# A recommendation tower on one core: another order for the first look-ups, table copies and grams, and a cap on the tables in flight

## The reference

```python
# dense_ctx (2048, 16), ids (2048, 27), tbl_f (1000 to 125000, 128), all float32
e = jnp.stack([tbl_0[ids[:, 0]], ..., tbl_26[ids[:, 26]]], axis=1)      # (2048, 27, 128)
dot_products = jnp.einsum('bnd,bmd->bnm', e, e)
z = dot_products[:, c, r]                   # the 351 pairs below the diagonal
h = jnp.concatenate([z, dense_ctx], axis=1)                             # (2048, 367)
h = jnp.maximum(h @ W_top1 + b_top1, 0.0)                               # 512 wide
h = jnp.maximum(h @ W_top2 + b_top2, 0.0)                               # 256 wide
y = h @ W_top3
```

## Time and profile before

| what | value |
|---|---|
| median of 3 runs | 360.65 us (360.56 to 360.74) |
| the profiled execution | 360.54 us |
| its span, first to last instruction | 358.7 us |
| TensorE busy | 333.7 us, 93% |
| VectorE, ScalarE, GpSimd busy | 246.3, 144.4, 250.4 us |
| mean granted TensorE clock | 0.986 of full speed |
| DMA moved | 36.86 MB |

### The profile page before, as it was taken

One profiled execution on the slowest core, in us unless ns is written; L12 is line 12 of the kernel. 1 busy time (PEld: TensorE's weight loads), 2 busy tenths in 40 slices (PEclk: granted clock), 3 DMA queues, 4 the chain that ended last, 5 costly groups with the idle time before them and its releaser, 6 DMA issues.

```text
span 358.7 us, 13616 instructions
## 1 busy us (share of the span) xinstructions
PE 333.7 (93%) x6094; PEld 303.4 (85%) x6094; DVE 246.3 (69%) x329; ACT 144.4 (40%) x265; POOL 250.4 (70%) x271
## 2 busy tenths in 40 slices
PE   1879699989999989999999999999999999999896
PEld 0779499978999979898889989999899989997775
DVE  3959979975488935878197965968387955961142
ACT  2536524444433433335343453435343353435320
POOL 5777777777777777777777777777777777777200
PEclk9969989999999999999999999999999999999999
DMA  6997744534333353443333452434533443322100
GB/s 184 306 318 196 205 136 107 102 93 91 83 93 82 90 99 75 96 96 80 93 88 82 115 85 77 105 84 81 102 89 83 99 98 74 84 55 55 27 3 1
DMA packets 26155, 36.86 MB, mean 103 GB/s; under 512 B 8451, under 2 KB 20099, under 8 KB 26098
## 3 DMA queue, kind: packets, MB, share of 16 engines
q0 software_dynamic: 8448, 17.32, 20.5%
q1 hardware_dynamic: 17506, 18.16, 20.1%
q10 hardware_dynamic: 144, 0.52, 0.4%
HBM read 35.97 MB, written 0.01 MB: 100 GB/s over the span
## 4 chain that ended last, share of the span: by engine, by line
PE 57%; POOL 26%; issue 10%; DVE 3%; DMA 3%; ACT 1%; DVEq 0%; ACTq 0%
POOL rows L450 26%; PE e_banks L482 25%; PE w_banks L543 9%; PE g_banks L513 8%; PE w_banks L554 7%; PE e_banks L494 6%; DMA rows<-in_tbl,idx 2%; DVE one_hot L672 2%; PE w_banks L532 1%; DVE zt L686 1%; DMA idx<-in_idx 1%; ACT et L340 0%; ACT h L333 0%; ACT et L350 0%; DVE a L720 0%
## 5 line engine op out<-in xcount | busy, mean ns | idle before, releaser
L450 POOL DMA_INDIRECT rows<-in_tbl,idx x264 | 249.6, 945 | 82.9 <-issue 78.0
L672 DVE TENSOR_TENSOR one_hot<-ids_wide,row_no 128x1024 fp32r<-128x1024 int32 x160 | 186.3, 1215 | 76.5 <-PE e_banks L482 72.5
L482 PE MATMUL e_banks<-one_hot,table_hi 128*128 128x256 f32 x672 | 172.2, 294 | 3.4 <-issue 3.4
L482 PE MATMUL e_banks<-one_hot,table_lo 128*128 128x256 f32 x672 | 167.0, 287 | 0.0
L482 PEld LDWEIGHTS e_banks<-one_hot,table_hi 128*128 128x128 f32 x672 | 131.4, 196 | 4.4 <-issue 4.2
L482 PEld LDWEIGHTS e_banks<-one_hot,table_lo 128*128 128x128 f32 x672 | 131.6, 196 | 0.2
L350 ACT ACTIVATE et<-e_banks 128x256 f32<-128x256 f32 x84 | 57.9, 689 | 89.3 <-PE e_banks L482 89.3
L340 ACT ACTIVATE et<-e_banks 128x512 f32<-128x512 f32 (+1 forms) x68 | 45.0, 664 | 52.3 <-PE e_banks L494 51.5
L513 PEld LDWEIGHTS g_banks<-et 128*26 128x26 f32 x4096 | 41.7, 103 | 17.7 <-issue 13.3
L513 PE MATMUL g_banks<-et 128*26 128x26 f32 x4096 | 50.0, 191 | 1.8 <-DVE zt L686 1.3
L494 PE MATMUL e_banks<-ident,rows 128*128 128x128 f32 x264 | 43.0, 285 | 5.5 <-DMA rows<-in_tbl,idx 5.5
(11 more groups left out here) (25 smaller groups left out, 67.7 us busy)
## 6 DMA issues: line engine op xcount, KB each, us to landing
ids_wide<-in_ids SPq DMA_DIRECT2D x80, 128.0 KB
et<-in_kept_tables SPq DMA_DIRECT2D x10, 512.0 KB, 10.1
rows<-in_tbl,idx POOLq DMA_INDIRECT x264
et<-in_kept_tables ACTq DMA_DIRECT2D x1, 512.0 KB, 3.9
a1T<-in_ids SPq DMA_DIRECT2D x4, 128.0 KB, 10.8
w<-in_w SPq DMA_DIRECT2D x2, 256.0 KB
w<-in_W_top SPq DMA_DIRECT2D x1, 512.0 KB
w<-in_w SPq DMA_DIRECT2D x1, 222.0 KB
```

What stands on the lines that cost most here:

```text
L450: pool.indirect_dma_start(rows[:, k % RING, a, :], None, tables[f], bass.IndirectOffsetOnAxis(ap=idx[:, t, f:f + 1], axis=0)).then_inc(row ...
L482: last = nc.tensor.matmul(e_bank[n % E_BANKS][:, 0:UNIT], part[:, q, c, :], one_hot[:, hot_slot(o, piece), c % PIECE, :], start=(c == 0 an ...
L672: nc.vector.tensor_tensor(one_hot[:, hot_slot(o, piece), :, :], ids_place(o).unsqueeze(1).broadcast_to([P, PIECE, UNIT]), row_no[:, piece ...
```

## The change

The six later look-ups of unit 0 are spread over the ticks 0 to 4, so the first of them now stands before chunk 1. The copy of the last table (HI 10) is moved out of the first look-ups to tick 6, behind half of tile 0's grams; it lies in `w_banks`, and the grams of tile 0 wait for the remainder of table 8, the last that reads `g_banks`, and no longer for a zeroed bank: the memset is gone. The grams of tile 0 stand in the ticks 5 and 6 instead of 6 to 9, and the look-ups of unit 1 move behind them. SyncE waits before table n until table n - 2 has landed. GpSimd waits before chunk k until chunk k - `ahead` is transposed, with `ahead` 3 for the first four chunks, 4 for the next four, and so on up to 7.

```diff
+LEAD_AT_FIRST = 3
...
     for n, q in enumerate(looked_up(0)):
-        at = 1 + (n - AHEAD) * 7 // 10
-        step = [("OH", 0, q)] + [("HI", n + AHEAD)]
-        if n == FIRST_LOOK_UPS - 1:
-            step += [("HI", m) for m in range(n + AHEAD + 1, NOH)]
+        step = [("OH", 0, q)] + ([("HI", n + AHEAD)] if n + AHEAD < NOH - 1 else [])
         if n < AHEAD:
             FIRST += step
         else:
-            look_ups[at].append(step)
+            look_ups[(n - 1) * 2 // 3].append(step)
+    look_ups[TILE_AT[1] + 1].append([("HI", NOH - 1)])
 
     for t in range(LAST_TILE):
-        at = TILE_AT[t + 1] + (t == 0)
+        at = TILE_AT[t + 1]
+        ticks = 2 if t == 0 else 4
         for p in range(G_PIECES):
...
-            grams[at + p * 4 // G_PIECES].append(step)
+            grams[at + p * ticks // G_PIECES].append(step)
...
-        hi_banks = [g_banks, w_banks]
+        hi_banks = [w_banks if n == NOH - 1 else (g_banks, w_banks)[n % 2] for n in range(NOH)]
+        LAST_IN_G = max(n for n in range(NOH) if hi_banks[n] is g_banks)
...
                     sp.wait_ge(hi_ready, n - STAGES + 1)
+                if n >= 2:
+                    sp.wait_ge(table_in[n - 2], 16)
                 sp.dma_start(stage(n), kept_tables[:, TABLE_ORDER[n], :, :]).then_inc(table_in[n], 16)
...
-                if k >= RING:
-                    pool.wait_ge(t_filled, k - RING + 1)
+                ahead = min(RING, LEAD_AT_FIRST + k // 4)
+                if k >= ahead:
+                    pool.wait_ge(t_filled, k - ahead + 1)
...
                 if t == 0 and p == 0:
-                    pe.wait_ge(g_banks_zeroed, 1)
+                    pe.wait_ge(lo_ready, LAST_IN_G + 1)
...
-                if n >= 2:
+                if n == NOH - 1:
+                    pe.wait_ge(lo_ready, n)
+                elif n >= 2:
                     pe.wait_ge(lo_ready, n - 1)
...
-                if n == NOH - 1:
-                    dve.wait_ge(lo_ready, NOH)
-                    nc.vector.memset(g_banks[:], 0.0).then_inc(g_banks_zeroed, 1)
```

More of the change, by code:

```diff
@@ L138, in dlrm_tower @@
         else:
-            look_ups[at].append(step)
+            look_ups[(n - 1) * 2 // 3].append(step)
+    assert FIRST_LOOK_UPS + AHEAD == NOH - 1
+    look_ups[TILE_AT[1] + 1].append([("HI", NOH - 1)])
     for t in range(LAST_TILE):
-        at = TILE_AT[t + 1] + (t == 0)
+        at = TILE_AT[t + 1]
+        ticks = 2 if t == 0 else 4
         for p in range(G_PIECES):
             step = [("G", t, p)] + ([("turn", t), ("pack", t)] if p == G_PIECES - 1 else [])
-            grams[at + p * 4 // G_PIECES].append(step)
+            grams[at + p * ticks // G_PIECES].append(step)
     for u in range(LAST):
@@ L163, in dlrm_tower @@
             look_ups[k].append([])
-        places = [(k, i) for k in ticks for i in range(len(look_ups[k]))]
+        places = [(k, i) for k in ticks for i, step in enumerate(look_ups[k]) if not step]
         for (k, i), q in zip(places, looked_up(u), strict=True):
@@ L293, in dlrm_tower @@
         ids_aside_in = {o: sem(f"ids_aside_in{o}") for o in range(IDS_RING, FIRST_LOOK_UPS)}
-        g_banks_zeroed = sem("g_banks_zeroed")
         table_in = [sem(f"table_in{q}") for q in range(NOH)]
@@ L564, in rounded_table @@
                 for i in range(OC * D // BANK):
-                    last = nc.tensor.matmul(hi_banks[n % 2][:, i, :], ident_r[:], upper[:, i * BANK:(i + 1) * BANK],
+                    last = nc.tensor.matmul(hi_banks[n][:, i, :], ident_r[:], upper[:, i * BANK:(i + 1) * BANK],
                                             start=True, stop=True)
@@ L656, in keep_rest @@
                                         stage(n).rearrange("p c d -> p (c d)"),
-                                        hi_banks[n % 2][:, :, :].rearrange("p k d -> p (k d)"),
+                                        hi_banks[n][:, :, :].rearrange("p k d -> p (k d)"),
                                         ALU.subtract).then_inc(lo_ready, 1)
-                if n == NOH - 1:
-                    dve.wait_ge(lo_ready, NOH)
-                    nc.vector.memset(g_banks[:], 0.0).then_inc(g_banks_zeroed, 1)
             def make_one_hot(o):
```

## The result

| | kernel before | kernel after |
|---|---|---|
| median | 360.23 us (20 runs, 359.51 to 361.94) | 361.25 us (20 runs, 359.89 to 364.22) |
| ratio to before | | 1.0026, 95% interval 1.0015 to 1.0038 |
| the profiled execution, its span | 360.54, 358.7 us | 362.27, 360.5 us |

The time lies inside the predicted range, half a microsecond above the predicted 360.7. But the kernel before came out at 360.23 beside it, so the change itself is 1.0 us, where the prediction had none. The side was wrong: the kernel is 0.26% slower, most of the interval lies above the 0.2% that the prediction called a change, and the prediction gave that 0.14. The same kernel in another set of runs gave 1.0023 (1.0010 to 1.0037).

A forecast was written before the change was run, and what follows sets the result against it. The prediction took GpSimd's fixed gather pace to chunk 24, that chunk's landing, and 227 us of TensorE work behind it as the bound; every part of the change summed to 0, giving 360.7 us, range 360.1 to 362.0.

The forecast's parts named there:

- GpSimd's pace absorbs the early gain: Gathers start every 1.25 us without a stop, so TensorE's 4 us early gain is lost before chunk 14: value 0.
- still come at 79.53: Chunk 14's last gather is still issued at 75.63, so its rows come when they did before the change.
- Waits on GpSimd and SyncE at no cost: Both new waits priced 0: gather 12 has 1.9 us margin; table 3 lands at about 15, upper bound 1.8 us.
- Shifted by 3.5: VectorE's one-hots and remainders start at 19.8 instead of 23.32, so remainder 9 ends at about 40.7.
- doubted that shorter queues bring rows sooner: Early chunks: DMA engines take turns between rings, so fewer queued tables give gathers no larger share; worth 0 either way.
- The fit that the prediction takes from the Trainium skill: Table DMA time as 2 us plus bytes over 436 GB/s: 3.2 us for a table alone, where 3.9 was seen.
- First look-up of unit 1 at 42.6: On TensorE, this look-up starts at about 42.6 instead of 45.51, 2.9 us earlier.
- the idle time before chunk 14: TensorE's wait for rows there grows from 1.5 to 2.6 us, using up the early saving.
- rival 1: Longer idle before chunk 14 lowers TensorE's clock: +0.5 us (short, chance 0.20) or +2.1 us (long, 0.07).
- Rival 2: GpSimd held at gather 12 by a late table 3, moving all gathers: up to +1.8 us, 362.5; chance 0.06.
- The memset goes; it stood behind the last remainder and only frees VectorE: Removing VectorE's memset before unit 1 was taken to cost nothing on the path.
- from 79.53 on order and work are the same: From chunk 14 on nothing changes, so the new order's value is 0.

The follow-up runs named there:

- late_pad: Kernel after plus a small extra VectorE memset, with the weights asked for only once chunk 6 is transposed: 360.57 us, ratio 1.0009.
- weights_late: Kernel after with the weights asked for once chunk 6 is transposed instead of chunk 4: 361.82 us, ratio 1.0025.
- two_fewer: Kernel before without two of its 264 gathers, the last of chunk 8 and of chunk 9: 358.2 us, ratio 0.9944.
- order_only: Kernel after without SyncE's wait and with GpSimd 7 chunks ahead from the start, leaving new order and missing memset: 361.9 us, ratio 1.0028.
- before_cap: Kernel before with SyncE's new wait alone added: 360.68 us, ratio 0.9986.
- no_cap: Kernel after without SyncE's new wait: 362.32 us, ratio 1.0038.
- pad_again: Repeat of the kernel after with a small extra VectorE memset behind the last table's lower half: 360.45 us, ratio 1.0014.
- before_nomemset: Kernel before without the VectorE memset of g_banks: 361.86 us, ratio 1.0013.
- late_grams: Kernel after with the grams of tile 0 back in ticks 6 to 9: 362.6 us, ratio 1.0043.
- after_pad: Kernel after with a small extra VectorE memset of 8 elements behind the last table's lower half: 360.57 us, ratio 0.9987.
- after_again: Kernel after once more, unchanged: 360.84 us, ratio 1.0023.

## Where the prediction was right and where it was wrong

*GpSimd's pace absorbs the early gain: right, and shown.* The last gather stands at 333.1 as predicted. Chunk 24 stands at 131.67 (predicted 131.6), though by another wait than the one foreseen, so that the number agrees better than the account of it; `late_pad` and `weights_late` show the gain reaching chunk 7 and being absorbed, `two_fewer` shows that fewer gathers are worth something, and the late start of `order_only` that a late queue costs its full 1.8 us. One reading was too firm: the rows of chunk 14 do not "still come at 79.53". With its last gather issued within half a microsecond in all but one profile (75.32 to 75.84), TensorE took them, after a wait, at 78.05 (`weights_late`) to 79.79 (`before_cap`).

*Waits on GpSimd and SyncE at no cost: right.* Gather 12 at 19.40 was not held, table 3 was rounded at 15.25 (predicted about 15), and `before_cap` and `no_cap` put SyncE's wait at nothing that can be measured. GpSimd's wait was not run alone; `order_only`, which drops it, has the ratio 1.0028 against 1.0038 with it, and the intervals overlap.

*"Shifted by 3.5" by the new order alone: right in the number, and half by luck.* VectorE's remainder of the last table but one starts at 39.8 us, 3.3 us before the 43.1 of the kernel before. But `before_cap`, in the old order, has it at 39.5 and `no_cap` at 40.2, so either part of the change does nearly all of it, and at chunk 4 it is mostly SyncE's wait. The prediction gave that wait no effect and doubted that shorter queues bring rows sooner; `before_cap` has the rows of chunk 1 at 18.59 instead of 20.42. The fit that the prediction takes from the Trainium skill, DMA: Bandwidth & Descriptors, Anatomy of one DMA, is given there for DMAs that GpSimd issues. The table that took 3.9 us was issued on ScalarE's queue, so 3.2 against 3.9 is no test of it. In the sum all this is worth 0 either way.

*First look-up of unit 1 at 42.6: wrong, harmless.* It came at 46.99. The sum had shifted TensorE's and VectorE's work by 3.5 us and left out what this triggers: the weights wait for chunk 4, are asked for 3.7 us earlier, and land among the rows of chunks 5 and 6. `weights_late` shows it (43.31). Hence the idle time before chunk 14 stayed at 1.49 us instead of 2.6, chunk 13 stayed at 74.83 instead of 73.7, and rival 1 (a long idle time there lowers the clock) was never put to the test. Rival 2 did not come either. These two give the range its upper end of 362.0, so that 361.25 lies inside it is in part luck. The low clock came at 41.5 us instead, under the same cover.

*"The memset goes; it stood behind the last remainder and only frees VectorE": the step that failed.* With it fell what "from 79.53 on order and work are the same" was to give, the same time. The order is the same, but each later instruction of VectorE stands one place earlier in its program, and VectorE then starts a one-hot at 159 us 0.36 us later than its wait allows. This delays the turn of a tile and so the pairs that TensorE waits for, 0.35 us: shown, by taking the memset out of the kernel before and by putting a stand-in into the kernel after. The prediction had priced this at 0 and had no rival for it. It cost the side, not the range.

*What holds VectorE up: not shown, with one clue.* The traces record the packets that bring instructions. On the queue that the page lists as "q14 instruction" a packet of 8 KB starts at 156.0 to 157.9 us in the seven kernels with the memset or a stand-in, before the one-hot in question, and at 160.7 to 162.8 in the seven without, 1.2 to 1.5 us behind its late start. Another starts at 245 to 247 against 252 to 255 us, around the second late start. The rest of this queue's packets behind 150 us do not move in this way. So late starts and packets move together. Whose instructions these packets hold, and that VectorE waits for them, no run here shows.

*The rest is in the grams, and its cause is open.* Between chunks 24 and 67 the grams take 33.2 us in the kernel after and 32.4 in the kernel before. The 64 weight loads of the two pieces of grams in a tick take 0.63 us, but some take up to 0.87. TensorE's weight loads in order of time, 263 to 275 us, in `pad_again` and then in `before_nomemset`:

```profile
264.00 0.63 PEld L525 LDWEIGHTS g_banks<-et 128*26 128x26 f32 x64
268.92 0.63 PEld L525 LDWEIGHTS g_banks<-et 128*26 128x26 f32 x64 [0.33 <-issue]
273.80 0.63 PEld L525 LDWEIGHTS g_banks<-et 128*26 128x26 f32 x64 [0.33 <-issue]
```

```profile
264.00 0.84 PEld L512 LDWEIGHTS g_banks<-et 128*26 128x26 f32 x64
269.10 0.87 PEld L512 LDWEIGHTS g_banks<-et 128*26 128x26 f32 x64 [0.33 <-issue]
274.23 0.74 PEld L512 LDWEIGHTS g_banks<-et 128*26 128x26 f32 x64 [0.33 <-issue]
```

TensorE is at the same place at the same time, and loses 0.21, 0.24 and 0.11 us in three grams in a row. The kernel after, `no_cap`, `late_grams` and `after_pad` lose at the same three grams (`after_pad` at two of them), `after_again`, `order_only` and `weights_late` do not. So these losses are not fixed by VectorE's instruction count, and how much of them the memset causes was not separated from chance of the execution.

*How firm the link to the times is.* The late start at 159 us is beyond doubt in the traces. In the times, the three kernels nearest to the question without memset stand at 1.0026, 1.0023 and 1.0013, the three with the stand-in at 0.9987, 1.0014 and 1.0009, and the single intervals overlap. Taken together they say more. `after`, `after_again` and `weights_late` (38 runs) lie 0.25% above the kernel before of their own sets, the same kernels with the stand-in, `after_pad`, `pad_again` and `late_pad` (30 runs), 0.08%, with an interval from -0.01 to 0.18%. The difference is 0.17%, 0.05 to 0.29% by resampling the recorded times, or 0.6 us (0.2 to 1.1). So the stand-in gives back about two thirds of the loss, and the interval takes in the 0.35 us that is traced. The sets ran on different chips, and the one pair on the same chip, `after_again` and `pad_again`, does not settle it alone. Part of the loss may also be executions in which chunks 14 and 24 come late (`late_grams`); in the kernel after, one run of 20 took 364.22.

## What to carry to other kernels

Before an early gain is counted, look for the queue with a fixed pace (here GpSimd: 1.25 us a gather, no stop) and for the first wait on it; nothing saved ahead of that wait arrives, while gathers left out, or a queue that starts late, do. When an early stage moves forward, list every transfer that it releases, and place these among the transfers that are on time now. And at effects of a quarter of a per cent, an instruction taken out is not free: compare the long stretch behind the change, which has no wait for rows, in both traces, and put a harmless instruction in the old one's place before the order is blamed. Where an idle time is put down to another engine, look also for the end of the wait itself.

## What the hardware showed that I had not expected

One VectorE instruction more or less, some 110 us earlier in its queue, decides whether VectorE starts the same one-hot 0.04 or 0.40 us after its wait has ended (7 profiles against 7). TensorE's train of small weight loads, at the full clock, loses 0.1 to 0.24 us in single grams, and which grams these are differs between kernels and between executions of one kernel. A table of 512 KB takes 5.5 us with at most two in flight and 10.1 without that limit (medians), and the last of the eleven landed at 33.0 and 32.4 us.
